# Cross-attention kernel: the matmuls outside the weighted sum issued as four 32-column tiles

## What is computed

```python
Q, K, V = (hidden @ Wq.T), (a @ Wk.T), (a @ Wv.T)       # per head: 16 columns
scores = einsum('bhtd,bhsd->bhts', Q, K) * scale
out = einsum('bhts,bhsd->bhtd', softmax(scores), V)
x = hidden + tanh(gate) * (out @ Wo.T)                  # layer 0
hidden = out @ cproj_w + cproj_b + residual             # layer 1
x = hidden + gelu(layer_norm(hidden) @ fc_w + fc_b) @ proj_w + proj_b
```

## Time and profile before

| | |
|---|---|
| Median of 3 runs | 2083.75 us (2082.23 to 2087.56) |
| The profiled execution, its own time | 2077.01 us |
| Its span, first to last instruction | 2075.2 us |
| Mean granted TensorE clock, share of full speed | 0.976 |
| TensorE matmul busy | 1970.8 us, 95% |
| VectorE busy | 1414.9 us, 68% |
| ScalarE busy | 1260.5 us, 61% |
| GpSimd busy | 423.2 us, 20% |

### The profile page before, as it was taken

How to read it: one execution, slowest core, us unless ns; L and a number is a source line. 1 busy time by engine, 2 the same in 40 slices (tenths; PEclk the granted TensorE clock), 3 DMA queues, 4 the chain that set the end, 5 groups by cost and what they waited for, 6 DMA issues and landing times.

```text
span 2075.2 us, 45909 instructions
## 1 busy us (share of the span) xinstructions
PE 1970.8 (95%) x14940; PEld 1057.2 (51%) x14940; DVE 1414.9 (68%) x2389; ACT 1260.5 (61%) x2327; POOL 423.2 (20%) x441
## 2 busy tenths in 40 slices
PE   6899989999999999999999999999999999999996
PEld 4345545454545545555554555445554454554544
DVE  3677777777667775777767676676766777676752
ACT  2266656667556675666656675566655667565673
POOL 2041113103221132311232022310223102111110
PEclk8799999999999999999999999999999999999998
DMA  5525151433215152151422415133241424214100
GB/s 149 139 66 148 52 149 37 110 89 106 73 51 130 57 143 63 33 148 45 129 64 65 137 30 148 41 96 105 71 108 43 114 81 118 61 53 116 29 2 11
DMA packets 142780, 176.84 MB, mean 85 GB/s; under 512 B 35092, under 2 KB 113085, under 8 KB 140469
## 3 DMA queue, kind: packets, MB, share of 16 engines
q1 hardware_dynamic: 140373, 170.67, 30.5%
q10 hardware_dynamic: 2144, 2.90, 0.6%
HBM read 125.33 MB, written 48.16 MB: 84 GB/s over the span
## 4 chain that ended last, share of the span: by engine, by line
PE 70%; issue 9%; SPq 7%; DVE 5%; POOL 3%; ACT 3%; DMA 2%; POOLq 0%; DVEq 0%; ACTq 0%
PE p_acc L1150 16%; PE p_sc L1117 16%; PE p_mx L1137 13%; PE p_misc L1185 8%; PE p_misc L1178 4%; SPq L489 3%; PE p_misc L1211 3%; SPq L502 2%; PE p_misc L1223 2%; PE p_misc L1171 2%; DVE maxes L872 2%; DMA scr_k<-parts 1%; POOL parts L625 1%; DVE rest L952 1%; PE p_misc L1217 1%
## 5 line engine op out<-in xcount | busy, mean ns | idle before, releaser
L872 DVE TENSOR_REDUCE maxes<-p_mx 128x1 f32<-128x802 f32 x1024 | 984.1, 983 | 349.5 <-PE p_mx L1137 346.5
L782 ACT ACTIVATE prob<-p_sc 128x512 f32<-128x512 f32 (+1 forms) x1664 | 923.9, 595 | 382.7 <-PE p_sc L1117 371.4
L1117 PE MATMUL p_sc<-qst,kst 100*128 100x256 bf16 (+1 forms) x3328 | 651.1, 278 | 39.3 <-ACT prob L782 28.3
L1137 PE MATMUL p_mx<-kst,qst 97*128 97x401 bf16 x2048 | 530.6, 341 | 10.9 <-DVE maxes L872 9.8
L1150 PE MATMUL p_acc<-prob,vals 128*17 128x256 f32 x6656 | 526.1, 388 | 7.7 <-ACT o_raw L790 7.4
L1117 PEld LDWEIGHTS p_sc<-qst,kst 100*128 100x128 bf16 (+1 forms) x3328 | 263.0, 100 | 526.4 <-ACT prob L782 228.0
L625 POOL TENSOR_TENSOR parts<-rest,parts 128x512 bf16<-128x512 f32 (+1 forms) x144 | 139.5, 969 | 649.4 <-DVE parts L963 649.3
L1150 PEld LDWEIGHTS p_acc<-prob,vals 128*17 128x17 f32 x6656 | 110.7, 95 | 252.6 <-issue 191.0
L1137 PEld LDWEIGHTS p_mx<-kst,qst 97*128 97x128 bf16 x2048 | 193.6, 99 | 55.7 <-DVE maxes L872 27.1
L1185 PE MATMUL p_misc<-wv,ctxt 128*128 128x256 f32 x800 | 193.7, 384 | 2.0 <-DVE rest L952 2.0
L1178 PE MATMUL p_misc<-ctxt,wk 128*128 128x512 f32 x488 | 190.7, 513 | 1.1 <-ACT vals L736 0.7
(11 more groups left out here) (143 smaller groups left out, 1083.9 us busy)
## 6 DMA issues: line engine op xcount, KB each, us to landing
kst<-scr_k SPq DMA_DIRECT2D x384, 200.1 KB
scr_k<-parts SPq DMA_DIRECT2D x96, 384.0 KB, 2.9
ctxn<-in_ctx_dram SPq DMA_DIRECT2D x16, 1536.0 KB
qst<-scr_q SPq DMA_DIRECT2D x384, 32.0 KB, 2.5
scr_q<-parts SPq DMA_DIRECT2D x16, 384.0 KB, 3.0
xin<-in_x_dram SPq DMA_DIRECT2D x8, 256.0 KB, 2.7
out_dram<-y SPq DMA_DIRECT2D x8, 256.0 KB, 2.1
scr_k<-parts SPq DMA_DIRECT2D x32, 48.8 KB, 2.0
```

The lines of the kernel that those rows point to most:

```text
L782: act.activation(prob[0:rows, u % 2, 2 * half:2 * half + 2, :].rearrange("p h t -> p (h t)"), p_sc[0:rows, half, :], ACT.Exp).then_inc(exp ...
L872: dve.tensor_reduce(maxes[:, c:c + 1], p_mx[:, c % 2, :, 0:CW], AX.XY, ALU.max).then_inc(chunk_done, 1)
L1117: ins = mm(p_sc[0:rows, half, T * q:T * q + T], kst[0:RB, h, P * j:P * j + rows], qst[0:RB, h, :], start=True, stop=True)
L1137: ins = mm(p_mx[:, c % 2, w, 0:CW], qst[0:RA, h, P * t:P * t + P], kst[0:RA, h, s0:s0 + CW], start=True, stop=True)
```

## The change

A helper `mm4` cuts one matmul by its result partitions (the columns of the weights) into up to four matmuls of 32 result partitions each. All of them read the same moving operand in full. `scores`, `chunk` and the pieces K, V, Q, WO, FC and PJ call `mm4` in place of `mm`. The transposes (T, XT, HT, MX), `weigh` and the matmuls of the setup are as they were. Waits and signals are as they were, with the signal on the last of the four.

```diff
+            def mm4(into, weights, moving, start, stop):
+                rows = weights.shape[-1]
+                for r0 in range(0, rows, P // 4):
+                    r1 = min(r0 + P // 4, rows)
+                    ins = mm(into[r0:r1, :], weights[:, r0:r1], moving, start=start, stop=stop)
+                return ins
...
-                    ins = mm(p_sc[0:rows, half, T * q:T * q + T], kst[0:RB, h, P * j:P * j + rows],
-                             qst[0:RB, h, :], start=True, stop=True)
+                    ins = mm4(p_sc[0:rows, half, T * q:T * q + T], kst[0:RB, h, P * j:P * j + rows],
+                              qst[0:RB, h, :], start=True, stop=True)
...
-                    ins = mm(p_mx[:, c % 2, w, 0:CW], qst[0:RA, h, P * t:P * t + P], kst[0:RA, h, s0:s0 + CW],
-                             start=True, stop=True)
+                    ins = mm4(p_mx[:, c % 2, w, 0:CW], qst[0:RA, h, P * t:P * t + P], kst[0:RA, h, s0:s0 + CW],
+                              start=True, stop=True)
...
-                        ins = mm(res[:, 0:w], wk[blk.prep][:, c, P * mo:P * mo + P], rhs,
-                                 start=(c == 0), stop=(c == CH - 1))
+                        ins = mm4(res[:, 0:w], wk[blk.prep][:, c, P * mo:P * mo + P], rhs,
+                                  start=(c == 0), stop=(c == CH - 1))
...
```

More of the change, by code:

```diff
@@ L1184, in do_piece @@
                         for c in range(CH):
-                            ins = mm(res[0:r, o:o + D], ctxt[:, j, c, 0:r], wv[blk.prep][:, c, :],
+                            ins = mm4(res[0:r, o:o + D], ctxt[:, j, c, 0:r], wv[blk.prep][:, c, :],
                                      start=(c == 0), stop=(c == CH - 1))
@@ L1203, in do_piece @@
                         for c in range(CH):
-                            ins = mm(res[:, T * mo:T * mo + T], wq[blk.prep][:, c, P * mo:P * mo + P],
+                            ins = mm4(res[:, T * mo:T * mo + T], wq[blk.prep][:, c, P * mo:P * mo + P],
                                      y[:, c, :], start=(c == 0), stop=(c == CH - 1))
@@ L1210, in do_piece @@
                     for g in range(NG):
-                        ins = mm(res[:, 0:D], o_t[:, g, P * t:P * t + P], wo[blk.post][:, g, :],
+                        ins = mm4(res[:, 0:D], o_t[:, g, P * t:P * t + P], wo[blk.post][:, g, :],
                                  start=(g == 0), stop=(g == NG - 1))
@@ L1216, in do_piece @@
                         for c in range(CH):
-                            ins = mm(res[:, T * a:T * a + T], wfc[:, c, P * f:P * f + P], x_t[:, c, :],
+                            ins = mm4(res[:, T * a:T * a + T], wfc[:, c, P * f:P * f + P], x_t[:, c, :],
                                      start=(c == 0), stop=(c == CH - 1))
@@ L1222, in do_piece @@
                     for f in range(FT):
-                        ins = mm(res[:, 0:D], g_t[:, f, P * t:P * t + P], wpj[:, f, :],
+                        ins = mm4(res[:, 0:D], g_t[:, f, P * t:P * t + P], wpj[:, f, :],
                                  start=(f == 0), stop=(f == FT - 1))
```

## The result

| | before | after |
|---|---|---|
| Median | 2083.72 us (4 runs) | 2068.97 us (4 runs, 2061.48 to 2075.82) |
| Ratio | | 0.9932, 95% interval 0.9912 to 0.9952 |
| Profiled execution, span | 2075.2 us | 2074.0 us |
| Mean granted TensorE clock | 0.976 | 0.958 |
| Matmul busy | 1970.8 us, 95% | 1865.8 us, 90% |

The kernel is 0.7% faster, where 7% was forecast; 2069 us lies outside the range of 1890 to 2020 us.

What follows compares the result with a forecast made beforehand. TensorE was taken to set the pace, losing about 0.1 us per tiling-mode change. Profiled 2077 - 186 + 30 (VectorE) + 4 (jumps) = 1925 us, plus 6.7 us to the median: 1932 us, 7% faster; range 1890 to 2020 us.

Steps and rivals of the forecast that it cites:

- points 1 to 6 of the sum: TensorE's path: mode changes around `weigh`, MX and transposes, first scores' weights, K pieces of 65 columns; together 186 us off.
- The term for the loop's jump: At the loop's jump back, fewer instructions' worth of work queued ahead: 0.7 us more each, five times, 4 us.
- Behind T, which the sum had as before: Mode changes now come before the 127 transposes, costing 11 us; behind them nothing changes.
- the price of tiled steps: 32-column bf16 steps on four tiles priced at nothing; 161 us if their weight loads were never hidden.
- 30 us of new waits: VectorE's reductions only partly covered by two `p_mx` buffers: 30 us come back, with 10 and 60 as ends.
- What comes back as waits: Part counting time given back: 30 us of VectorE waits, none for ScalarE, 4 us at the loop's jumps.
- the sentence on ScalarE: First exponential of a unit takes 1.10 us against 1.22 until needed; other work follows longer pieces, so ScalarE just fits.
- 34 were forecast: Waits that come back: 30 us for VectorE and 4 us at the loop's jumps.
- the rival of late instructions: Issue becomes the bound of TensorE, as fetching falls behind: 2100 to 2500 us; chance 0.13.
- The rate that I feared: In plain units, 32 load and matmul pairs slow things if each costs over 45 ns; at 60 ns, some 390 us more.
- one packet for 6 us: Instruction packets rise from 137 to about 340: one per 6 us on average, one per 4.5 in plain units.
- the prediction's own list of signs that it is wrong: Scores steps over 0.11 us, TensorE idle with "issue" inside a unit, or VectorE and ScalarE idle time growing past 100 us.

Runs made afterwards that it cites:

- experiment 9: Changed kernel with keys of group 0 loaded at unit 22, its queries at 24, group 1 at 37, group 2 at 40: 2007.6 us, ratio 0.9656.
- experiment 13: Changed kernel with keys/queries loaded at units 22/24, 37, 40, key loads of 64 columns and maxima over half the columns (work left out): 1955.3 us, ratio 0.9416.
- experiment 1: Changed kernel with the second load of keys and queries issued at unit 37 instead of 26, behind the K stores: 2026.5 us, ratio 0.972.
- experiment 14: Changed kernel with keys of group 0 loaded at unit 22, its queries at 24, group 1 at 37, group 2 at 49: 1986.3 us, ratio 0.9551.
- experiment 15: Changed kernel with loads at units 22 (group 0 keys), 24 (its queries), 37, 40, and V as full-array matmuls: 1988.8 us, ratio 0.9577.
- experiment 4: Changed kernel with the 256 moving columns of each scores matmul issued as two times 128, 26,000 more instructions: 2087.1 us, ratio 1.0036.
- experiment 6: Changed kernel with key loads after the prologue moving only 64 of 1601 columns, work left out: 2042.2 us, ratio 0.9824.

## Why the prediction was wrong

The kernel is at 2069 us where 1932 were forecast, 137 us more. By the ratios, the order of the loads is 57 us of this (experiment 9), small key loads and half the maxima together 50 more (experiment 13), and 30 are left. Neither SyncE's queue nor late instructions inside a unit have a term in the sum.

**Right: what the change does to TensorE** (points 1 to 6 of the sum). 186 us were forecast, and the small gaps fell by 176. The term for the loop's jump was right too: the gap there grew from 2.1 to 2.2 us to 2.6 to 3.1, five times, 3.4 us together where 4 were forecast. Behind T, which the sum had as before, `weigh` comes 0.05 us later. That the loss goes with the change between 128 and 32 columns, and that MX with its 24 columns falls on the tiled side, stands in the rows; that the tiles' weight loads are hidden shows in a step of scores that stays at 0.11 us with four of them, whose matmuls start 6 to 8 ns apart. The Trainium skill's sentence that changing the tiling mode drains TensorE (TensorEngine Tiling (Array Packing), Key Properties) holds here, in both directions: 0.1 us went wherever a change went, and 0.11 us came where one came.

**Mis-sized, slightly: the price of tiled steps.** I took nothing; streaming at full clock rose by 20 us over 7616 steps, 2.6 ns each.

**In the sum, and of the right order: VectorE.** 30 us of new waits were forecast. TensorE's waits for the maxima rose from 36.9 to 70.5 us. But half the maxima also gain 0.5% in the kernel before, so of the 1.0% only half belongs to the change: some 10 us, with intervals that allow 1 to 20. As half of the reductions' work was left, the whole may be more; that 30 us is right isn't shown.

**Wrong: "What comes back as waits".** I asked which engine would be full next, and counted VectorE and ScalarE. The step that failed is the sentence on ScalarE: "Its other work follows pieces, in which TensorE spends more." It holds for ScalarE's own time. But its `parts` operation also waits for a store, that store waits for SyncE's queue, and SyncE takes 0.6 us for each of the 13 loads that stand right in front, 26 with the group ahead of them, whatever TensorE does. No queue was in my sum, though SPq stood in the chain before with 7%. Long gaps grew by 118 us, where 34 were forecast. Experiments 1 and 9 show SyncE's order behind 44 to 57 us of the time; in the trace of experiment 9 that is 42 us of long gaps and 29 us of half clock.

**Half wrong: the rival of late instructions.** It had 0.13 and a time of 2100 to 2500 us. The rate that I feared is no problem: 32 pairs of load and matmul fit into a plain unit of 1.23 us, 38 ns each. The Trainium skill's 62 ns for each matmul without the hardware's decoding (TensorE: Matmul & The Clock Gate, Part 1) isn't seen here. What happens is rarer: 29 bare stalls, 34 us, most of them beside the traffic of loads. I had an average, one packet for 6 us, where the dense units beside the traffic counted. "Issue" inside a unit was on the prediction's own list of signs that it is wrong, and it came.

**Left out: the clock.** Half clock cost 38 us before and 74 after; the sum has no term for it. It follows long gaps: of 27 gaps over 2.5 us in the changed kernel (from 100 us on), 21 had half clock inside them or right behind them, six had not. With the loads in order and the same instructions it is at 45 (experiment 9), with fewer bare stalls at 31 to 38 (experiments 14, 15).

**What stays open.** With SyncE's order, traffic and VectorE out of the way 1955 us are left (ratio 0.9416) against the forecast 1932 (0.927), 1.4% or 30 us. In the traces, over the whole span, small gaps fell by 182 us, longer steps cost 20, half clock 7, and long gaps grew by 33. That the last is near the forecast's 34 of waits is luck: those were meant for VectorE, and here half of its reductions are left out. The 126 us of long gaps of experiment 13 lie at units 0, 51, 22 and 35 above all; units 0 and 51 have the loop's jump and the end of the kernel. Apart from the jumps I didn't take these apart. The orders of experiments 9 and 14 were not run in the kernel without tiles, so how much of the 4.5% such an order alone would give is open; the one move tried there gave 0.55%. That late instructions are the cause of the bare stalls rests on experiments 4, 6 and 15 (more instructions, less traffic, fewer instructions) and on the packets, behind whose ends the stalls end; what in the traffic delays the packets isn't shown.

## What to carry to other kernels

Where column tiles and full-array matmuls alternate, count the changes and price them from the start-to-start times: here about 0.1 us each, 176 us in all. Before you book such a gain, go through every queue that keeps its own time, not only the engines: list for each DMA queue what stands in front of a store or a load that an engine will want earlier, because a queue that issues at 0.6 us apiece doesn't speed up with the engine it serves. Here the tiles were worth 0.7% with the loads where they were and 2.3% with one group of loads moved in both kernels; tiles and three moved groups together gave 4.5%.

## What the runs showed of the hardware that I had not expected

- Two kernels that differ in one unit of the place of a load (21 or 22) differ by 3.7%: at 21 the load is issued ahead of the store of the maxima, and TensorE waits 65.5 us for them, at 22 behind it, and it waits 6.5 us.
- A key load takes as long to issue with 64 columns as with 1601: 0.595 us in the median of 384 in both, and ScalarE's waits for the stores behind them were 80.6 us against 71.2.
- Instructions of TensorE came late mostly beside the traffic of the loads: bare stalls of 34 us with the full key loads, 5 us with small ones, at 313 packets in both. Such a stall ended 1.2 to 1.75 us behind the end of an instruction packet, all 39 of them in the changed kernel.
- The jump back of the loop left TensorE without matmuls for 2.1 to 2.2 us in the kernel before, 2.6 to 3.1 in the changed one, and 3.9 to 4.7 where a group of loads stood at the jump (experiment 14).
- The granted clock fell to half (1.2 GHz of 2.4) behind most gaps over 2.5 us (21 of 27), so that a gap can cost more than its own length: the changed kernel spent 177 us at half clock against 102 before.
